# Two layers of cross-attention on one core: single products of the maxima set between the products of the queries' projection

## The reference, cut to what matters

```python
q = hidden_state @ Wq + bq                 # 32 heads of 16
k = encoder_hidden_state @ Wk + bk         # 8 heads of 16
v = encoder_hidden_state @ Wv + bv
scores = jnp.einsum('bkgld,bksd->bkgls', q, k) * scale + mask
attn = jax.nn.softmax(scores, axis=-1)
out = jnp.einsum('bkgls,bksd->bkgld', attn, v)   # heads put together again
x = out @ Wo + bo + hidden_state
mu = jnp.mean(x, axis=-1, keepdims=True)
var = jnp.var(x, axis=-1, keepdims=True)
return (x - mu) * jax.lax.rsqrt(var + EPS) * gamma + beta
```

## Time and profile before

| | |
|---|---|
| median of 3 runs | 1835.99 us (1834.97 to 1836.72) |
| the profiled execution | 1835.3 us, of which the span of its instructions 1833.2 us |
| PE busy | 1779.6 us (97% of the span), 11521 records |
| PEld busy | 1153.3 us (63%) |
| DVE, ACT, POOL busy | 1370.1 us (75%), 1078.4 us (59%), 571.0 us (31%) |
| granted TensorE clock, mean | 0.985 |

### The profile page before, as it was taken

The page is one execution under the profiler, slowest core; times in us unless marked ns, Lnnn a source line. Parts: engine busy times, 40 slices in busy tenths (PEclk is TensorE's granted clock), DMA queues, the critical chain, the costliest instruction groups (busy, mean ns, idle before and its releaser), DMA issues. The chain is left out here.

```text
span 1833.2 us, 37386 instructions
## 1 busy us (share of the span) xinstructions
PE 1779.6 (97%) x11521; PEld 1153.3 (63%) x11521; DVE 1370.1 (75%) x1808; ACT 1078.4 (59%) x2530; POOL 571.0 (31%) x1165
## 2 busy tenths in 40 slices
PE   4899999999999999999999999999999999999996
PEld 3566566666666666666666666666666666666652
DVE  6577677777777777777777777787777777777784
ACT  1465565666656656656656656656665656656653
POOL 1232233323323323323323323323323333333321
PEclk8899899999999999999999999999999999999997
DMA  8346445445445445445445445444444444444431
GB/s 288 100 121 180 130 125 137 129 120 140 129 121 139 132 117 142 133 115 144 133 119 144 128 109 135 128 111 133 128 114 131 126 116 127 125 126 117 129 82 42
DMA packets 200894, 235.92 MB, mean 129 GB/s; under 512 B 41706, under 2 KB 176100, under 8 KB 199812
## 3 DMA queue, kind: packets, MB, share of 16 engines
q1 hardware_dynamic: 180356, 205.82, 40.0%
q10 hardware_dynamic: 20480, 29.38, 6.9%
HBM read 101.39 MB, written 22.02 MB: 67 GB/s over the span
## 5 line engine op out<-in xcount | busy, mean ns | idle before, releaser
L627 DVE TENSOR_REDUCE mx<-ms 112x2 f32<-112x750 f32 x1024 | 933.4, 933 | 412.6 <-PE ms L758 401.1
L500 ACT ACTIVATE probs<-sc 125x448 f32<-125x448 f32 x1536 | 751.5, 542 | 344.5 <-PE sc L741 337.0
L758 PE MATMUL ms<-ks,qs 96*112 96x375 bf16 x2048 | 501.0, 326 | 10.4 <-DMA qs<-qp 7.8
L741 PE MATMUL sc<-qs,ks 99*125 99x448 bf16 x1536 | 423.6, 356 | 11.1 <-DMA qs<-mT 8.3
L758 PEld LDWEIGHTS ms<-ks,qs 96*112 96x112 bf16 x2048 | 254.7, 131 | 223.5 <-issue 114.4
L777 PE MATMUL pv<-probs,vs 125*32 125x448 f32 x3072 | 317.4, 546 | 0.0
L741 PEld LDWEIGHTS sc<-qs,ks 99*125 99x125 bf16 x1536 | 199.5, 138 | 127.5 <-ACT probs L500 75.3
L819 PE MATMUL job<-wo,on 128*112 128x512 f32 x512 | 268.6, 607 | 7.2 <-POOL on L442 5.7
L841 PE MATMUL job<-xT,wq 128*128 128x112 f32 x2048 | 249.9, 276 | 0.0
L841 PEld LDWEIGHTS job<-xT,wq 128*128 128x128 f32 x2048 | 245.2, 193 | 3.5 <-issue 0.6
L456 POOL TENSOR_TENSOR kr<-kf,kp 128x375 f32<-128x375 f32 x64 | 57.5, 899 | 534.5 <-ACT kp L537 534.5
(11 more groups left out here) (54 smaller groups left out, 999.1 us busy)
## 6 DMA issues: line engine op xcount, KB each, us to landing
ctxT<-in_ctxT SPq DMA_DIRECT2D x64, 750.0 KB, 5.8
qs<-qp SPq DMA_DIRECT2D x768, 56.0 KB, 2.7
ks<-kp SPq DMA_DIRECT2D x768, 46.9 KB, 2.5
osum<-oraw ACTq DMA_DIRECT2D x128, 112.0 KB, 2.8
oc<-oraw ACTq DMA_DIRECT2D x128, 112.0 KB, 3.4
mask<-in_mask SPq DMA_DIRECT2D x64, 164.1 KB, 2.3
xT<-in_xT SPq DMA_DIRECT2D x32, 224.0 KB, 6.5
xin<-in_x SPq DMA_DIRECT2D x32, 224.0 KB, 6.6
```

The source lines that it names most:

```text
L500: nc.scalar.activation(probs[0:KCS, k, j, :], sc[j][0:KCS, 0:GL], ACT.Exp)\
L627: nc.vector.tensor_reduce(mx[o][:, 2 * j:2 * j + 2], ms[j % 2][0:S, :, 0:S2], AX_X, ALU.max)\
L741: last = nc.tensor.matmul(sc[j][0:KCS, 0:GL], ks[p][0:KM, g, rows], qs[p][0:KM, g, :], start=True, stop=not masked)
L758: last = nc.tensor.matmul(ms[j % 2][0:S, n, 0:S2], qs[o][0:KT, g, S * c:S * c + S], ks[o][0:KT, g, :], start=True, stop=True)
```

## The change

Three things. `PAIRS_AT` moves one pair from piece 1 to piece 5 and one from piece 3 to piece 6, so that pieces 5 and 6 have two pairs each and pieces 1 and 3 one. In pieces 5 and 6 the pairs no longer stand ahead of or behind the products of the queries: `project_queries` takes the numbers of the pairs and sets one product of the maxima after the first, third, fifth and seventh of its eight products. A pair then waits for `max_done` at its first product and reports at its second. DVE's reciprocals get a condition `step == 0`, so that a piece with two reductions still has one reciprocal, between the two.

```diff
-PAIRS_AT = [2, 2, 1, 2, 0, 1, 1, 1, 2, 2, 1, 1]
+PAIRS_AT = [2, 1, 1, 1, 0, 2, 2, 1, 2, 2, 1, 1]
...
-                            if k == 5 and p_ok:
+                            if k == 5 and step == 0 and p_ok:
                                 reciprocal(1)
...
-                    def maximum(j):
-                        if j % (PAIRS // 2) == 0:
+                    def maximum(j, of=(0, 1)):
+
+                        if 0 in of and j % (PAIRS // 2) == 0:
                             pe.wait_ge(stack[o][2 * j // PAIRS], 16 * NSTACK * (ahead + 1))
-                        if j >= 2:
+                        if 0 in of and j >= 2:
                             pe.wait_ge(max_done[o], PAIRS * ahead + j - 1)
-                        elif m_ok:
+                        elif 0 in of and m_ok:
                             pe.wait_ge(max_done[p], PAIRS * main + PAIRS - 1 + j)
-                        for n in range(2):
+                        for n in of:
...
-                        last.then_inc(ms_ps[o], 1)
+                        if 1 in of:
+                            last.then_inc(ms_ps[o], 1)
...
-                    def project_queries(heads):
+                    def project_queries(heads, maxima):
...
+                                n = DC * (c - heads[0]) + t
+                                if n == 2 * DC - 1 and NG - 1 in heads:
+                                    last.then_inc(q_ps[p], 1)
+                                if n % 2 == 0 and n // 4 < len(maxima):
+                                    maximum(maxima[n // 4], (n % 4 // 2,))
...
-                        next_maximum()
+                        if k not in (5, 6) or not j_ok:
+                            next_maximum()
...
                         if k == 5 and j_ok:
-                            project_queries((0, 1))
+                            project_queries((0, 1), list(pairs))
...
                         if k == 6 and j_ok:
-                            project_queries((2, 3))
+                            project_queries((2, 3), list(pairs))
```

More of the change, by code:

```diff
@@ L691, in slot @@
                                 result_rows()
-                            if k == 4 and p_ok:
+                            if k == 4 and step == 0 and p_ok:
                                 reciprocal(0)
-                            if k == 5 and p_ok:
+                            if k == 5 and step == 0 and p_ok:
                                 reciprocal(1)
-                            if k == 6 and p_ok:
+                            if k == 6 and step == 0 and p_ok:
                                 reciprocal(2)
-                            if k == 7 and p_ok:
+                            if k == 7 and step == 0 and p_ok:
                                 reciprocal(3)
@@ L842, in project_queries @@
                                                         start=(t == 0), stop=(t == DC - 1))
+                                n = DC * (c - heads[0]) + t
[3 more added lines that the diff above has]
+                                    maximum(maxima[n // 4], (n % 4 // 2,))
                         if NG - 1 in heads:
-                            last.then_inc(q_ps[p], 1)
                             job_free[0] = (q_evac[p], NG * (proj + 1))
```

## The result

| | before | changed |
|---|---|---|
| median of 20 runs each | 1835.87 us | 1833.01 us |
| lowest and highest | 1833.80, 1837.95 | 1829.24, 1837.11 |
| span of the profiled execution | 1833.2 us | 1830.9 us |

The ratio is 0.9982, with a 95% interval of 0.9976 to 0.9989. The change is a gain, of about 3.3 us, clear of the noise. 8.2 us were forecast, and 1833.0 lies above the range of 1820.5 to 1832.

The account below looks back on a forecast made before the run. PE's own sequence was taken as the bound. Gains of 0.128 + 0.016 less 0.01, rounded to 0.13 us a slot, times 63 gave 8.2 us: 1827.5 us forecast, range 1820.5 to 1832.

Parts of the forecast that it names:

- The bound: Whole slot: PE busy 27.63 of 27.68 us in layer 0; only shorter PE start-to-start distances shorten a slot.
- Heads of runs: Pieces 5 and 6: four more runs each follow a maxima product, gaining 0.016 us each, 0.128 a slot.
- A product of the maxima behind the queries: Pieces 5 and 6: the last queries' record before a maxima product still costs 0.11 us, nothing gained or lost.
- Pairs split: Pieces 5 and 6: maxima products standing singly gain 0.004 us for each of four pairs, 0.016 a slot.
- The moved pairs: Pieces 1 and 3 lose 0.32 us each, 5 and 6 gain it: net nothing, plus 0.01 added in piece 3.
- what hides the waits: Pieces 5 and 6: DVE's about 2.6 us per piece just fits; piece 5 becomes 2.73 us.
- no new idle of PE before the maxima: Changed profile: if the forecast is right, PE gains no new idle time ahead of the maxima products.
- The margins of DVE: Tightest waiter, piece 6's second pair, has 0.4 us to spare; piece 3 loses at most 0.05 before the scores' exponentials.
- The sum: 0.128 + 0.016 - 0.01 = 0.134, rounded down to 0.13 us a slot, times 63 slots: 8.2 us.
- DVE comes too late: Rival: piece 5's second reduction ends too late; 0.3 us beyond the margin per slot gives +10.7, 1847 us; chance 5%.

Follow-up runs that it names:

- The kernels with four extra heads: Two kernels: old table, pairs of pieces 5 and 6 split among the queries' products, 1832.78 us; changed kernel with pairs kept whole inside the queries' run, 1835.83 us.
- The narrow weights: Queries' products use 96 of 128 weight columns: on the kernel before 1809.96 us, ratio 0.9856; on the changed kernel 1813.73 us, ratio 0.9876.
- the table alone: Kernel before with the new PAIRS_AT, each pair whole and ahead of or behind the queries' run: 1839.84 us, ratio 1.0020.
- both other kernels with the crowded slot and 128 weight columns: New table with pairs whole at the ends of the queries' run, 1839.84 us; changed kernel with pairs whole inside that run, 1835.83 us.
- single products alone: Changed kernel with the old PAIRS_AT, so one split pair each in pieces 5 and 6: 1832.78 us, ratio 0.9980.
- the last slot mended: Changed kernel with the old table where no queries' projection exists: 1831.14 us, ratio 0.9968; also with second scores product behind the second queries' product: 1827.52 us, ratio 0.9954.

## Why the prediction was wrong, point by point

**The bound.** Right. PE's own sequence is the slot, and steady slots changed only by PE's distances from start to start.

**Heads of runs.** Right in mechanism, and nearly in size. 0.016 for each of eight heads was forecast. Added up over 16 slots of layer 0, the queries' products take 3.433 us a slot in the change and 3.559 before, 0.126 less or 0.0158 a head, where 0.128 was forecast. The kernels with four extra heads give 0.064 / 4 = 0.016 and 0.062 / 4 = 0.0155. The narrow weights show what it hangs on. The rule of the Trainium skill ("TensorE: Matmul & The Clock Gate", What overlaps and what doesn't) that a load overlaps only where the row group differs, weighed in the prediction, is not what the trace shows: all 176 heads of runs behind a maxima product on shared row groups between 200 and 800 us had their lead, with a first turn of 0.098 to 0.100.

**A product of the maxima behind the queries.** Right: 0.111 or 0.112 behind four records (0.109 behind two, as in a run's second turn), not 0.095.

**Pairs split.** This is the first of the two steps that failed: a term of the sum that was mis-sized, and with the wrong sign. My range allowed a gain of 0 to 0.02 a pair and no loss. I read the second product's 0.158 as what any product costs that is followed by queries, and gained 0.004 a pair. In truth the first of its kind pays about 5 ns whatever follows, and a single product is always the first: 0.163 + 0.163 against 0.162 + 0.158, 0.006 more a pair. Four pairs make +0.024 instead of -0.016 a slot (added up, the maxima's products take 0.025 more), 63 x 0.040 = 2.5 us. The unrounded starts would have shown that the interval goes with the product ahead, since scores have it too, 0.193 and 0.188.

**The moved pairs.** "Nothing", and 0.01 in piece 3: right for the steady slots, the table alone costs 0.007. Wrong for the one slot that I left out of the account. The second step that failed is **what hides the waits**: the cover of DVE's 2.6 us in pieces 5 and 6 is the projection of the queries, and I said how much of it there is, but not in which slot it is missing. In the last slot with maxima pieces 5 and 6 are two scores products and two pairs each. PE waits 1.73 us for DVE there, which makes its waits in these pieces some 1.2 us longer than before, and the fallen clock adds about 1.5: 2.8 us in all. The sign "no new idle of PE before the maxima" fails there too.

**The margins of DVE.** Right in the slots with a projection. In layer 1 of the changed kernel the second reduction of piece 5 starts late, behind the reciprocal, and yet the product that waits for it comes well after:

```profile
1451.63 0.88 DVE L627 TENSOR_REDUCE mx<-ms 112x2 f32<-112x750 f32 x1
1452.76 0.94 DVE L627 TENSOR_REDUCE mx<-ms 112x2 f32<-112x750 f32 x1 [0.25 <-PE ms L759]
...
1452.99 0.33 PE L759 MATMUL ms<-ks,qs 96*112 96x375 bf16 x1
```

It is over at 1452.5, and the first product of piece 6's second pair starts at 1452.99, 0.5 later, where 0.4 was reckoned. PE lost nothing before the scores of piece 4 either: its waits for the exponentials are 1.7 us in the whole execution, and were 2.4.

**The sum.** 8.2 forecast, less 2.5 for the split pairs is 5.7, the steady slots' 5.8; less 2.8 for the last slot is 2.9, the measured 2.9 to 3.3. The rival "DVE comes too late" had the right engine and the wrong slots: I priced it 63 times or not at all, and the right count was one. In the range, a lead of 0.020 gives 63 x 8 x 0.020 = 10.1 us, not 10.5, which changes nothing here.

## What to carry to other kernels

Where a run of products is paced by its weight loads, each long stream set into it saves once about the difference between load and stream, and the separator can be any product that is there anyway; but a product taken out of its pair costs a few ns, so count both.

When work is moved under a cover, list the slots in which that cover does not exist (first, last, layer change), and give each its own table: here one slot of 64 ate half the gain.

Read distances of a few ns from unrounded starts, sorted by what stands ahead and by what follows, before giving them a cause.

## What the runs showed of the hardware that was not expected

A product behind one of another shape takes 3 to 5 ns more than one behind its like: scores 0.193 and 0.188 us, maxima 0.162 and 0.158, transposes 0.098 and 0.095. It holds between two bf16 products of 99 and 96 rows, and it doesn't go with the load that follows. Rows, columns and streamed columns all change with the shape here, and so do the tensors that are loaded and streamed; which of them it is was not tried and stays open.

A short wait can cost more than itself. In the last slot 1.73 us of waiting for DVE, in two gaps, were followed by 3.41 us at the lower clock in the changed kernel, and by the same 3.41 in both other kernels with the crowded slot and 128 weight columns. In the kernel before, whose waits there were 0.45, 0.29 and 0.18 us, in the one with single products alone and in the ones with the last slot mended the clock stayed at its upper level there. Long waits for DVE are not the only way to it. Where scores and maxima alternate, the table is the old one and the waits for ScalarE were much like those before, 0.44, 0.46 and 0.18 us, and yet the clock was low for 6.83 us in that slot, right behind them. How much waiting it takes, and whether chance has a part in it, is not shown.
